# Grouped attention in a new order on all engines of one Trainium2 core

## The chip, the core and the metric

One NeuronCore of one Trainium2 chip runs the whole program. The metric is the device time of one execution in microseconds (us). The core has five engines with a queue each: PE (matrix products and transposes), DVE (vector work), ACT (activations and copies), POOL (vector work and indexed DMAs) and SP (DMA issue). Each takes its own instructions in order; semaphores tie the queues together.

## What is computed

Four layers of attention and feed-forward follow one another over 2048 tokens of width 256. The change touches only the last attention, the grouped one of layer 3 (16 query heads, 4 key and value heads of 64, 77 context tokens). Cut to what matters:

```python
h = _layernorm(x)
Q = rope(h @ Wq)                      # 16 heads of 64
K, V = rope(ctx @ Wk), ctx @ Wv       # 4 heads, each used by 4 query heads
scores = Q @ K.T * 64**-0.5 + rel_pos_bias[:, |i - j|]
x = x + (softmax(scores) @ V).reshape(...) @ Wo
x = x + experts(_layernorm(x))        # 8 experts, one per token, 320 places each
```

## The kernel before, in words

`attn_gqa` holds this attention as one stage. Tokens are cut into 16 tiles of 128 (`NT` is 16, `HALF` is 8). `K` and `V @ Wo` were prepared earlier (`KB`, `VW`), so that a tile needs these links:

- ln: layer norm of a tile, then `lnT`, two transposes on PE, and `lnT_copy` on ACT;
- `queries`: 128x1024 products into two PSUM banks, as two halves of 512 columns;
- `rope` on DVE (three operations from PSUM into `t1`, `t2`), the addition into `qr` on POOL, `q_transpose` (8 transposes on PE), `qT_copy` (two copies on ACT);
- `scores` on PE, `shift` on DVE (adds the bias, takes the maximum of each head, subtracts it), `exps` on ACT, `sums` on DVE (sum of each head and the reciprocal `rden`), the multiplication by `rden` on POOL (`p_ok`);
- `prob_transpose` on PE (ten transposes in three groups of 4, 4 and 2, through the two banks of `ring`), `pT_copy` on ACT, `output` on PE (ten products of `pT` with `VW` into `bank_y`), `residual` on DVE (adds `bank_y` into x, `x_ok`), and `bn_stats` for the next layer norm.

Beside that, DVE adds the results of the previous experts into tiles ahead of their use (`add_experts`), computes variances for groups of four tiles (`variance`, `inverse`; ACT takes the square root in `deviation`), and from tile 8 on prepares the next layer's routing: the normalised tiles `lnk` (`route`), and `first_expert`, `first_slot` and `slots` (`places`). PE has its share of this in `route` (transposes of `lnk`, logits, ranks), and `keep_warm` issues matrix products whose results nobody reads.

Nothing is scheduled by a program: each engine's function `step(t, q)` is an order written out by hand, called for t up to `NT`, in which tiles t-1 to t+7 are worked on at different links. In the step of PE before, these are `scores(t)`, `prob_transpose(t-1)`, `lnT(t+2)`, `output(t-1)`, `q_transpose(t+1)`, `route(t)`, `queries(t+2)`. "Step t" below is the stretch of PE from the first product of `scores(t)` to the first of `scores(t+1)`.

## Time and profile before

| | us |
|---|---|
| median of 3 runs (lowest, highest) | 1019.61 (1019.53, 1022.49) |
| span of the profiled execution | 1018.8 |
| the grouped attention in it | from 573.0 to 806.9 |
| PE busy over the span | 905.3 (89%) |
| DVE busy over the span | 722.6 (71%) |
| ACT busy over the span | 379.2 (37%) |
| POOL busy over the span | 376.2 (37%) |

The span runs from the first to the last instruction of one execution that the profiler recorded. What that same execution took as a whole is not given; the median of the runs lies 0.8 above the span. The lines L... are those of the kernel before. In a timeline, a row gives the start, the length of the group, engine, line, operation, the names written and read, and in brackets for how long the engine had sat idle and what ended it; of a group of several (x8) the ends are modelled, so that distances between starts are the safer reading. The trace counts an f32 product of PE twice (8 products are x16), a transpose once.

### The profile page before, as it was taken

What the parts mean: (1) busy time and instruction counts of PE and PEld (TensorE: products, weight loads), DVE (VectorE), ACT (ScalarE), POOL (GpSimd) and SP (SyncE); (2) the same over time, 40 slices, a digit from 0 to 9 for tenths busy, and PEclk for the clock granted to TensorE, in tenths of its full rate; (3) what the DMA queues carried; (4) which work ended last, traced back from release to release, by engine and by line L of the source; (5) the groups of instructions that cost most, each with busy time, mean ns of one, the idle gap of its engine ahead of it and who ended that gap; (6) DMA issues with size and microseconds to landing.
All of it is one profiled execution on the core that took longest, in us unless ns stands there. A gap on an engine that the chain in (4) does not pass through costs nothing. (4 is left out here: it accounts for less than half of the span.)

```text
span 1018.8 us, 17183 instructions
## 1 busy us (share of the span) xinstructions
PE 905.3 (89%) x5832; PEld 642.5 (63%) x5832; DVE 722.6 (71%) x1632; ACT 379.2 (37%) x862; POOL 376.2 (37%) x279
## 2 busy tenths in 40 slices
PE   2899989999889976868899889999999839999997
PEld 2788743444478864733578467776767517777787
DVE  6799968887699979878377799999989731222221
ACT  3466640000156556844355143434343303122222
POOL 1676404333577623427355223333324410110111
PEclk9999999999999997979999999999999959999999
DMA  7100079999200009002465651111111284624200
GB/s 224 40 1 0 1 223 306 318 324 310 115 1 1 0 2 270 2 27 106 135 197 166 207 173 51 50 50 31 45 50 40 73 313 168 207 89 163 92 12 20
DMA packets 87258, 117.16 MB, mean 115 GB/s; under 512 B 12464, under 2 KB 75949, under 8 KB 86781
## 3 DMA queue, kind: packets, MB, share of 16 engines
q1 hardware_dynamic: 77455, 88.15, 28.5%
q10 hardware_dynamic: 4408, 15.46, 4.3%
q0 software_dynamic: 5328, 12.70, 3.5%
q8 instruction: 38, 0.62, 0.3%
q14 instruction: 29, 0.24, 0.1%
HBM read 68.08 MB, written 50.16 MB: 116 GB/s over the span
## 5 line engine op out<-in xcount | busy, mean ns | idle before, releaser
L1016 PE MATMUL psum<-m_W,lnT 128*128 128x512 f32 x256 | 114.3, 599 | 1.2 <-DVE acc L928 1.2
L410 POOL TENSOR_TENSOR prob<-prob,a_rden 128x1232 f32<-128x1232 f32 x30 | 67.4, 2248 | 59.8 <-DVE a_rden L506 59.8
L1016 PEld LDWEIGHTS psum<-m_W,lnT 128*128 128x128 f32 x256 | 47.3, 190 | 59.5 <-issue 55.9
L2884 ACT ACTIVATE prob<-psum,x_b 128x320 f32<-128x320 f32 x64 | 33.7, 527 | 124.3 <-PE psum L2938 124.3
L2554 PE MATMUL psum<-g_VW,pT 128*128 128x256 f32 (+1 forms) x320 | 72.9, 383 | 1.8 <-ACT pT L2449 1.0
L2938 PE MATMUL psum<-x_xT,x_w 128*128 128x320 f32 x256 | 72.7, 444 | 1.3 <-DVE x_xT L2811 1.3
L1001 POOL TENSOR_TENSOR m_masked<-m_rel,m_mrow 128x1232 f32<-128x1232 f32 x16 | 42.3, 2644 | 82.9 <-DMA masked_bias<-m_masked 62.2
L2744 POOL DMA_INDIRECT out_x<-x_yt,x_X x20 | 19.8, 992 | 140.8 <-DVE x_yt L2825 140.8
L2554 PEld LDWEIGHTS psum<-g_VW,pT 128*128 128x128 f32 (+1 forms) x320 | 59.6, 190 | 12.2 <-issue 4.6
L2938 PEld LDWEIGHTS psum<-x_xT,x_w 128*128 128x128 f32 x256 | 49.6, 195 | 22.9 <-issue 4.4
L2221 POOL TENSOR_TENSOR g_qr<-g_t 128x1024 f32<-128x1024 f32 x15 | 35.4, 2359 | 76.0 <-DVE g_t L2298 76.0
L2228 POOL TENSOR_TENSOR prob<-prob,g_rden 128x1232 f32<-128x1232 f32 x15 | 33.7, 2248 | 73.8 <-DVE g_rden L2334 73.8
L2505 PE MATMUL psum<-g_Wq,lnT 128*128 128x512 f32 x128 | 57.9, 595 | 0.5 <-ACT lnT L2427 0.5
L2951 PE MATMUL psum<-x_w,prob 128*128 128x256 f32 x256 | 56.6, 379 | 0.0
L1389 POOL DMA_INDIRECT routed_results<-pT,m_idx x39 | 38.4, 984 | 39.4 <-DVE pT L1722 21.6
L401 POOL TENSOR_SCALAR ln<-x_tiles,mean,rstd 128x256 f32<-128x256 f32 x32 | 41.5, 1299 | 28.7 <-DVE rstd L433 27.0
L2951 PEld LDWEIGHTS psum<-x_w,prob 128*128 128x128 f32 x256 | 48.1, 190 | 6.1
L472 DVE TENSOR_TENSOR prob<-psum,mx 128x616 f32<-128x616 f32 x64 | 48.2, 795 | 3.0
L466 DVE TENSOR_REDUCE mx<-psum 128x16 f32<-128x1232 f32 x32 | 45.6, 1424 | 4.6 <-PE psum L632 3.6
L931 DVE SCALAR_TENSOR_TENSOR acc<-psum,gates,acc 128x256 f32<-128x256 f32 x96 | 40.4, 477 | 9.7 <-PE psum L1016 9.7
L2822 DVE TENSOR_TENSOR x_yt<-psum,x_b 128x256 f32<-128x256 f32 (+1 forms) x24 | 10.2, 424 | 52.3 <-PE psum L2951 41.3
L110 PE MATMUL psum<-RQ,identb 128*128 128x512 bf16 x135 | 32.5, 396 | 15.7 <-DMA expert_rows<-x_tiles,acc 12.8
(463 smaller groups left out, 2108.1 us busy)
## 6 DMA issues: line engine op xcount, KB each, us to landing
routed_rows<-hole SPq DMA_DIRECT2D x8, 2210.0 KB, 33.9
masked_bias<-m_masked ACTq DMA_DIRECT2D x16, 616.0 KB, 7.4
g_bias<-masked_bias SPq DMA_DIRECT2D x16, 616.0 KB, 3.8
x_w<-in_L_ffn_w SPq DMA_DIRECT2D x16, 512.0 KB, 4.6
x_w<-in_L_ffn_w SPq DMA_DIRECT2D x8, 1024.0 KB, 7.8
m_xb<-routed_rows SPq DMA_DIRECT2D x39, 130.0 KB, 2.2
...
expert_rows<-hole SPq DMA_DIRECT2D x1, 4680.0 KB, 33.5
```

Of the source, the lines that this page charges most:

```text
L401: nc.gpsimd.tensor_scalar(c.ln[b][:, :], xt(c, i), mean_of(c, i), rstd_of(c, i), ALU.subtract, ALU.mult).then_inc(ln_ok, 1)
L410: nc.gpsimd.tensor_tensor(heads(c.prob[b]), heads(c.prob[b]), rden[b][:, :].unsqueeze(2).to_broadcast([P, H, SK]), ALU.mult).then_inc(norm ...
L466: nv.reduce_max(c.mx[:, :].rearrange("p (r h) -> p r h", r=GROUPS), sview.rearrange("p r (h k) -> p r h k", k=SK), AX).then_inc(mx_ok, 1)
L472: nv.tensor_tensor(c.prob[b].rearrange("p (r h k) -> p r h k", r=GROUPS, k=SK)[:, r], sview[:, r].rearrange("p r (h k) -> p r h k", k=SK), ...
L931: ins = nv.scalar_tensor_tensor(out=c.acc[o][:, :], in0=src, scalar=gate, in1=c.acc[o][:, :], op0=ALU.mult, op1=ALU.add)
L1001: nc.gpsimd.tensor_tensor(masked[i % 2][:, :, :], rel[i // 2 % 2][:, :, :], mrow[:, i % 2, :].unsqueeze(1).to_broadcast([P, HB, SK]), ALU. ...
L1016: last = nt.matmul(c.ps[p][:, :], c.lnT[b][:, k * P:(k + 1) * P], W[:, k, p * 512:(p + 1) * 512], start=(k == 0), stop=(k == KC - 1))
L1389: ng.indirect_dma_start(out=c.yd2, out_offset=bass.IndirectOffsetOnAxis(ap=idx[:, b % RING:b % RING + 1], axis=0), in_=yb[:, b % YR, :], i ...
L2505: last = nt.matmul(c.ps[3 + u][:, :], c.lnT[b][:, k * P:(k + 1) * P], Wq[:, k, u * 512:(u + 1) * 512], start=(k == 0), stop=(k == KC - 1))
L2554: last = nt.matmul(bank_y[:, 0:D], c.pT[b][0:w, j * P:(j + 1) * P], VW[0:w, i // HALF, j, :], start=(j == 0), stop=(j == NB - 1))
L2938: last = nt.matmul(c.ps[2 + m % 4][:, 0:CAP], w1[b][:, k, m * P:(m + 1) * P], xT[b][:, k, :], start=(k == 0), stop=(k == KC - 1))
L2951: last = nt.matmul(c.ps[6 + ch % 2][:, 0:D], hT[b][:, m, r * P:(r + 1) * P], w2[b][:, m, :], start=(m == 0), stop=(m == MH - 1))
```

## The change

Everything lies in `attn_gqa`. The work per tile stays the same but for three pieces: the layer norm of a tile moves from DVE to ACT (with `shifts`, minus mean times rstd, computed per group on DVE); of the 16 heads, the first 8 (`FUSED`) are no longer shifted by DVE but by ACT's exponential itself, one head at a time, which also gives their sums; and the orders of all engines are written anew. The deepest links start a step earlier (`queries(t+2)` is followed by `rope(t+2)` in the same step, layer norm and `lnT` are those of t+3), and `residual` runs a step later (`finished(t-2)`).

```diff
@@ DVE: step @@
+        def finished(i):
+
+            residual(i, i % 2)
+            dve.wait_ge(s["x_ok"], i + 1)
+            nv.tensor_copy(c.gap[:, i % 2:i % 2 + 1], c.ones[:, 0:1])
+            stats = nv.bn_stats(bst_of(c, i), xt(c, tile(i)))
+            if i + 2 in (HALF + 1, HALF + 5):
+                chain(stats)
+                variance(group_of((i + 2 - HALF) // 4)[1], s["r_ve_ok"])
+
         def step(t, q):
             b = q % 2
-            if inside(t + 1):
-                rope(t + 1, 1 - b)
+            if inside(t + 3) and t % 4 == 1:
+                inverse(GROUP_OF[t + 3])
+            if inside(t - 2):
+                finished(t - 2)
             if inside(t):
                 shift(t, q)
-            if inside(t + 7):
+            if inside(t + 2):
+                rope(t + 2, b)
+            if t >= -1 and inside(t + 7):
                 add_experts(range(4, 7) if t < 0 else (t + 7,))
             route(t)
             if inside(t):
                 sums(t, b)
-            if inside(t - 1):
-                residual(t - 1, 1 - b)
-                dve.wait_ge(s["x_ok"], t)
-            if inside(t + 3):
-                if t % 4 == 1:
-                    inverse(GROUP_OF[t + 3])
-                layer_norm(t + 3, 1 - b)
-            if inside(t - 1):
-                nv.tensor_copy(c.gap[:, b:b + 1], c.ones[:, 0:1])
-                stats = nv.bn_stats(bst_of(c, t - 1), xt(c, tile(t - 1)))
-                if t in (HALF, HALF + 4):
-                    chain(stats)
+            if t == NT:
+                finished(t - 1)
             if t % 4 == 0 and inside(t + 7):
                 variance(slice(*TILE_GROUPS[GROUP_OF[t + 7]]), s["ve_ok"])
-            if t in (HALF, HALF + 4):
-                variance(group_of((t - HALF) // 4)[1], s["r_ve_ok"])
             places(t)
-        for t in range(-1, NT + 1):
+        for t in range(-2, NT + 1):
             step(t, t % 4)
 
@@ ACT: exponentials @@
+        def exps(t, b, first, last):
+            rest = c.prob[b][:, FUSED * SK:HB * SK]
+            act.wait_ge(s["links"], 2 * t + 1)
+            for h in range(first, last):
+                p = c.prob[b][:, h * SK:(h + 1) * SK]
+                ins = na.activation(p, p, ACT.Exp, bias=c.mx[:, h:h + 1], accum_out=c.den[:, h:h + 1])
+                if h == FUSED - 1:
+                    ins.then_inc(s["fused_ok"], 1)
+                if h == OPENING - 1:
+                    act.wait_ge(s["shifted"], t + 1)
+                    na.activation(rest, rest, ACT.Exp).then_inc(s["exp_ok"], 1)
@@ ACT: step @@
-                deviation(GROUP_OF[t + 7])
-            if t in (HALF, HALF + 4):
+            if inside(t + 3):
+                layer_norm(t + 3, 1 - b)
+            if t in (HALF + 1, HALF + 5):
                 u = (t - HALF) // 4
                 _, ones8, _ = group_of(u)
                 act.wait_ge(s["r_ve_ok"], u + 1)
                 na.activation(c.std[:, ones8], c.ve[:, ones8], ACT.Sqrt).then_inc(s["r_std_ok"], 1)
                 na.activation(spare[:, :], c.ones[:, 0:1], ACT.Exp)
-        step(-2, 2)
+            if inside(t + 1):
+                qT_copy(t + 1, 1 - b)
+            if inside(t - 1):
+                pT_copy(t - 1, 1 - b, 0)
+            if inside(t):
+                exps(t, b, 0, OPENING)
+            if inside(t - 1):
+                pT_copy(t - 1, 1 - b, 1)
+            if inside(t):
+                exps(t, b, OPENING, FUSED)
+            if inside(t - 1):
+                pT_copy(t - 1, 1 - b, 2)
+            route(t)
+            if inside(t + 3):
+                lnT_copy(t + 3, 1 - b)
+            if t % 4 == 0 and inside(t + 7):
+                deviation(GROUP_OF[t + 7])
+        deviation(0)
+        step(-3, 1)
         deviation(1)
@@ PE: step @@
                 pe.wait_ge(s["s_used"], NT)
                 pe_ranks(c, r, 1, c.ps[0]).then_inc(s["r_pre_ps"], 1)
+            early = t == 0
+            if inside(t + 1) and not early:
+                q_transpose(t + 1, 1 - b)
+            if inside(t + 2):
+                queries(t + 2, b, 0)
+            if t == NT:
+                keep_warm(c, c.ps[3], 2)
             if inside(t - 1):
                 if t - 1 in (0, HALF):
                     pe.wait_ge(vw_in[t // HALF], 16 * 2)
-                if t == NT:
-                    keep_warm(c, c.ps[3], 2)
-                prob_transpose(t - 1, 1 - b)
+                prob_transpose(t - 1, 1 - b, 0)
+            if inside(t + 2):
+                queries(t + 2, b, 1)
+            if inside(t + 1) and early:
+                q_transpose(t + 1, 1 - b)
+            if inside(t - 1):
+                prob_transpose(t - 1, 1 - b, 1)
             if t == HALF + 7:
                 pe.wait_ge(s["r_lgT_ok"], 2)
                 pe_logits_back(c, r, 1, c.ps[4]).then_inc(s["r_back_ps"], 1)
-            if inside(t + 2):
-                lnT(t + 2, b)
             if inside(t - 1):
-                output(t - 1, 1 - b)
-            if inside(t + 1):
-                q_transpose(t + 1, 1 - b)
+                output(t - 1, 1 - b, 0)
+                prob_transpose(t - 1, 1 - b, 2)
             route(t)
-            if inside(t + 2):
-                queries(t + 2, b)
+            if inside(t - 1):
+                output(t - 1, 1 - b, 1)
+            if inside(t + 3):
+                lnT(t + 3, 1 - b)
+            if inside(t - 1):
+                output(t - 1, 1 - b, 2)
             back(t)
             if t == NT - 2:
                 keep_warm(c, c.ps[0], 10)
```

Further hunks: POOL adds `qr` for tile t+2 instead of t+1, and DVE does so itself for tiles 0 and 1 instead of tile 0 alone; the last shift and sum cover heads 8 to 15 only; and `output(t-1, u)` waits for the copy of its own part u of `pT`, where before all ten products waited for the last copy. `output(i, 0)` waits, as before, for `x_ok` of the tile before it.

How the orders move is shown at three places. PE, a regular step before (`g_KB` is `scores`, `prob` is `prob_transpose`, `ln` is `lnT`, `g_VW` is `output`, `g_qr` is `q_transpose`, `g_Wq` is `queries`), up to the next step's first row:

```order
-L2527 MATMUL psum<-g_KB,g_qT 128x154 x8
-L2544 MATMUL psum<-ident,prob 128x128 x9
-L2544 MATMUL psum<-ident,prob 80x128
-L2497 MATMUL psum<-ident,ln 128x128 x2
-L2554 MATMUL psum<-g_VW,pT 128x256 x10
-L2518 MATMUL psum<-ident,g_qr 128x128 x8
-L2505 MATMUL psum<-g_Wq,lnT 128x512 x4
-L2527 MATMUL psum<-g_KB,g_qT 128x154 x8
```

and the same in the change, where the transposes of `prob`, the halves of the queries and the parts of the output alternate:

```order
+L2548 MATMUL psum<-g_KB,g_qT 128x154 x8
+L2539 MATMUL psum<-ident,g_qr 128x128 x8
+L2525 MATMUL psum<-g_Wq,lnT 128x512 x2
+L2564 MATMUL psum<-ident,prob 128x128 x4
+L2525 MATMUL psum<-g_Wq,lnT 128x512 x2
+L2564 MATMUL psum<-ident,prob 128x128 x4
+L2574 MATMUL psum<-g_VW,pT 128x256 x4
+L2564 MATMUL psum<-ident,prob 128x128
+L2564 MATMUL psum<-ident,prob 80x128
+L2574 MATMUL psum<-g_VW,pT 128x256 x4
+L2517 MATMUL psum<-ident,ln 128x128 x2
+L2574 MATMUL psum<-g_VW,pT 128x256 x2
+L2548 MATMUL psum<-g_KB,g_qT 128x154 x8
```

The transposes of `qr` moved from behind `output` to right behind `scores`; ten products on `g_VW` in one piece became 4, 4 and 2 with other work between them.

DVE in the change, the end of a step whose number is a multiple of four and the start of the next (`den` is `sums`, `bst` to `var_eps` is `variance`, `g_shifts` ends `inverse`, the last row begins `shift`):

```order
+L2331 TENSOR_REDUCE den<-prob 128x8
+L2333 RECIPROCAL g_rden<-den 128x16
+L2261 TENSOR_TENSOR mean<-bst 128x4
+L2262 TENSOR_TENSOR var_eps<-bst 128x4
+L2263 TENSOR_TENSOR rstd<-bst 128x4
+L2264 TENSOR_SCALAR mean<-mean 128x4
+L2265 SCALAR_TENSOR_TENSOR var_eps<-var_eps 128x4
+L2267 SCALAR_TENSOR_TENSOR var_eps<-rstd,var_eps 128x4
+L2269 TENSOR_SCALAR var_eps<-var_eps 128x4
+L2275 RECIPROCAL rstd<-std 128x4
+L2276 SCALAR_TENSOR_TENSOR g_shifts<-mean,rstd 128x4
+L2314 TENSOR_TENSOR prob<-psum,g_bias 128x924
```

Before, `residual`, the reciprocal of the earlier group and the layer norm on `ln` stood between `g_rden` and `variance`; now `variance` follows at once, and `inverse` stands ahead of the next `shift` instead of at that step's end.

DVE in the change, the end of the stage (`prob<-prob,g_rden` scales the last tile, `L1157` to `L1187` are `first_slot` and `slots`, the rows on `psum` that write `x_tiles` are `residual`):

```order
+L2337 TENSOR_TENSOR prob<-prob,g_rden 128x616 x2
 L1157 COPY acc<-acc 128x8 x2
 L1158 TENSOR_SCALAR acc<-first 128x4
@@ -1115,9 +1102,12 @@
 L1186 TENSOR_TENSOR acc<-acc 128x4
 L1187 TENSOR_TENSOR acc<-acc 128x4
-L2326 TENSOR_TENSOR x_tiles<-x_tiles,psum 128x256
-L2401 COPY gap<-ones 128x1
-L2402 BN_STATS bst<-x_tiles 128x6
+L2325 TENSOR_TENSOR x_tiles<-x_tiles,psum 128x256
+L2384 COPY gap<-ones 128x1
+L2385 BN_STATS bst<-x_tiles 128x6
+L2325 TENSOR_TENSOR x_tiles<-x_tiles,psum 128x256
```

The residual of tile 14, which stood ahead of `L1157`, now stands behind `L1187`, next to that of tile 15.

## Rows read from the trace of the kernel before

**Rows 1.** Windows of stage: length, busy time by engine, clock, DMA share, GB/s.

```profile
613.65:706.03 92.38, 88.80 (x450) 66.73 (x448) 90.20 (x126) 33.51 (x60) 33.81 (x15) 1.00 0.15 49
706.03:789.31 83.28, 78.86 (x429) 59.94 (x428) 74.69 (x140) 33.18 (x68) 28.66 (x14) 1.00 0.13 42
789.31:806.90 17.59, 16.56 (x94) 12.72 (x93) 14.53 (x45) 4.96 (x12) 7.58 (x6) 1.00 0.13 46
```

**Rows 2.** Timeline, PE, tile 4's step: start, duration, idle before it.

```profile
640.00 2.26 PE L2527 MATMUL psum<-g_KB,g_qT 128*128 128x154 f32 x16
642.10 1.04 PE L2544 MATMUL psum<-ident,prob 128*128 128x128 f32 x8
...
643.45 0.44 PE L2544 MATMUL psum<-ident,prob 128*128 128x128 f32 x2 [0.31 <-ACT pT L2446]
...
644.50 4.56 PE L2554 MATMUL psum<-g_VW,pT 128*128 128x256 f32 x20
...
648.90 1.04 PE L2518 MATMUL psum<-ident,g_qr 128*128 128x128 f32 x8
...
649.77 3.60 PE L2505 MATMUL psum<-g_Wq,lnT 128*128 128x512 f32 x8
...
653.21 2.26 PE L2527 MATMUL psum<-g_KB,g_qT 128*128 128x154 f32 x16
```

**Rows 3.** Timeline, the other engines in the same step.

```profile
640.96 1.20 DVE L2296 TENSOR_TENSOR g_t<-psum,g_cos 128x1024 f32<-128x1024 f32 x1
...
643.28 1.11 DVE L2314 TENSOR_TENSOR prob<-psum,g_bias 128x924 f32<-128x924 f32 x1
...
643.44 2.37 POOL L2221 TENSOR_TENSOR g_qr<-g_t 128x1024 f32<-128x1024 f32 x1 [2.94 <-DVE g_t L2298]
...
646.28 1.44 DVE L2321 TENSOR_TENSOR prob<-prob,mx 128x1232 f32<-128x1232 f32 x1
647.63 0.48 DVE L2247 SCALAR_TENSOR_TENSOR x_tiles<-lnk,g_gate,x_tiles 128x256 f32<-128x256 f32 x1
...
649.13 1.44 DVE L2333 TENSOR_REDUCE den<-prob 128x16 f32<-128x1232 f32 x1
649.60 1.08 ACT L2433 ACTIVATE g_qT<-psum 128x512 f32<-128x512 f32 x2 [0.62 <-PE psum L2518]
...
650.60 0.25 DVE L2334 RECIPROCAL g_rden<-den 128x16 f32<-128x16 f32 x1
...
650.93 2.25 POOL L2228 TENSOR_TENSOR prob<-prob,g_rden 128x1232 f32<-128x1232 f32 x1 [5.13 <-DVE g_rden L2334]
```

**Rows 4.** Timeline, ACT, an exponential that also sums, earlier stage.

```profile
406.58 0.42 ACT L1773 ACTIVATE prob<-psum,b_nb,b_rstdA 128x77 f32<-128x77 f32 x1 [0.56 <-DVE b_nb L1480]
...
406.99 0.41 ACT L1773 ACTIVATE prob<-psum,b_nb,b_rstdA 128x77 f32<-128x77 f32 x1
```

**Rows 5.** Groups by line and form: a normalising ACTIVATE, a table load.

```profile
L1749 ACT ACTIVATE pT<-lnk,i_rnd,i_linv 128x256 f32<-128x256 f32 x16 | 8.6, 594 | 5.5 <-DVE i_linv L1423 5.5
...
L2439 ACT ACT_TABLE_LOAD x3 | 3.8, 1283 | 0.1
```

**Rows 6.** Lines L936 and L2279: duration ns min/median/max, first and last start.

```profile
L936 DVE TENSOR_TENSOR x_tiles<-x_tiles,acc x16: 424/726/2850, 156.0 to 269.7; 128x256 f32 x12, 128x256 f32<-128x256 f32 x4
L2279 DVE TENSOR_SCALAR ln<-x_tiles,mean,rstd x16: 320/2158/2166, 575.9 to 758.3; 128x256 f32<-128x256 f32 x16
```

**Rows 7.** Windows: results added for three tiles; the last slot computation.

```profile
585.38:588.99 3.61, 3.48 (x14) 2.08 (x15) 3.54 (x11) 1.09 (x2) 0.00 (x0) 1.00 1.10 350
801.69:805.57 3.88, 3.88 (x19) 3.47 (x20) 3.29 (x20) 0.90 (x3) 0.00 (x0) 1.00 0.00 0
```

**Rows 8.** Timeline, PE, value products of the last tile.

```profile
801.94 4.48 PE L2554 MATMUL psum<-g_VW,pT 128*128 128x256 f32 x20
```

**Rows 9.** Timeline and window, an earlier idle PE and its clock.

```profile
440.97 0.71 PE L1963 MATMUL psum<-ident,prob 128*77 128x128 f32 x2 [3.34 <-ACT prob L1773]
440.00:444.00 4.00, 2.56 (x6) 1.85 (x7) 3.42 (x18) 1.29 (x6) 0.00 (x0) 0.50 0.00 2
```

146 lines of the change are left out of this document (68 added, 78 removed).

## The prediction

> **What bounds the kernel now.** First the windows: in steps 2 to 8, 92.38 us or 13.20 a step, PE is busy for 88.8 and DVE for 90.2 [rows 1]; only PE and DVE can be the bound, and both nearly are. Then PE's timeline in step 4 [rows 2], to see where the step loses time. It starts at 640.00 and 653.21, so it is 13.21 long. Starts that follow each other without a wait give the pace: scores 2.10 (to 642.10), eight transposes 0.87 (648.90 to 649.77, so 0.11 each), output 4.40, queries 3.44 (649.77 to 653.21), and 12 further transposes at 0.11 are 1.31. Sum 12.11; the other 1.10 are waits for ACT's copies, before 643.45 and 644.50. Then the other engines [rows 3]: DVE runs without a gap, rope 2.32, bias and maximum 3.00 (643.28 to 646.28), shift 1.35, one tile of expert results 1.50, sum 1.47. PE is the bound with 1.10 a step to gain; DVE is 0.5 behind it.
>
> What follows counts time from 0 at the first product of `scores(t)`.
>
> **A regular step of the change.** DVE loses the layer norm, 2.16 in most steps [rows 6], and half of shift and sum, about 1.4; 9.3 are left. ACT gains a layer norm (0.59 in a like form) [rows 5] and eight exponentials with sums at 0.41 from start to start [rows 4] for half of the long one, some 3.5 more on an engine that is busy for 33.5 of 92.4 [rows 1]. On PE: `q_transpose` at 2.10, first half of queries at 2.97, transposes of prob at 4.69, second half to 6.84, transposes to 7.28, four products to 9.04, then 9.26, 11.02, 11.24, end at 12.1. ACT: copies of qT from 2.8 (a copy starts 0.7 behind its four transposes) [rows 2, 3], first copy of pT 5.4 to 6.0, two exponentials to 6.8, the other half's exponential to 7.4, second copy from 7.55, six exponentials 8.0 to 10.5, last copy to 10.9, wanted at 11.24. Every PE wait is covered, by 0.3 at the least: 12.11, a gain of 1.10. The loads of the bias on SP wait for the same bias part of `shift` as before and are a step ahead of their use: nothing. The new `shifts` are one small DVE operation per group: nothing where DVE has 2 us to spare.
>
> **The shared access of DVE and POOL.** A DVE operation with two SBUF inputs or the layer norm's tensor_scalar takes its own time alone and POOL's time when POOL is at work: 0.42 against 2.85, and 0.32 against 2.16 [rows 6]. In the step before, POOL's two additions (start 643.44 and 650.93) met DVE's PSUM operations and the layer norm [rows 3]. Now POOL's `qr` addition, 0.1 behind rope's end, meets `add_experts`, and its multiplication by `rden`, 0.33 behind the reciprocal, meets `variance`. I price each meeting at POOL's 2.3 (the distances in rows 3 give 2.36 and 2.25 by the same layer norm's 2.16). The bounds are nothing, if scalar_tensor_tensor doesn't collide, and the full 2.3; I take the full, since the nearest rows, tensor_tensor of x and acc, reach it.
> The Trainium skill ("SBUF — State Buffer", Who interferes with whom) states that a DVE instruction with two SBUF inputs contends with a GpSimd one that reads SBUF, whoever is second waiting for all of the first. By it the sum is the one below; without it 4.5 instead of 16.4. The trace agrees for tensor_tensor; no row has a scalar_tensor_tensor of that kind beside POOL.
>
> In a regular step this pushes the reciprocal to 13.9, `p_ok` to 16.5, or 4.4 of the next step, wanted at 4.69. Still covered; the gain holds in steps 2, 3, 4, 6, 7 and 8.
>
> **Steps after a multiple of four.** In step 4 `variance` waits for POOL (16.5) and ends at 17.4, 5.3 in step 5. ACT stands in `deviation` for it, and `inverse` and the layer norm on ACT now come before `qT_copy`: square root 5.6, inverse 6.0, layer norm 6.6, copy 7.0. PE wants the copy at 4.69: 2.4 lost. A table load of 1.28 [rows 5] and the late shift cost another 1.1 before the last part of output. Step 5 takes 15.6. Steps 2 to 8: six times 12.11 and 15.6 are 88.3 against 92.38: −4.1.
>
> **Start.** Before, step 2 starts at 613.65 [rows 1], and `add_experts` for three tiles runs from 585.38 to 588.99 [rows 7], right behind the addition for tile 0. In the change that addition ends at about the same time, 585.3; PE then needs 0.87 and 3.44 before tile 1's queries are there, at 589.6, and DVE, whose next instruction is rope(1), stands idle until then. Rope 2.3 and its own addition for tile 1 (estimate 1.2, half of POOL's 2.36) end at 593.2, the three tiles' 3.6 at 596.8. Then `shift(0)` with its bias part done at 598.3 and its end at 600.6, rope(2) to 602.9, POOL's addition, behind the scalar_tensor_tensor in flight, to 605.7. PE starts scores(1) at 598.3, has done them by 600.5 and waits 5.2 for that addition, with queries(3) and everything behind in its queue. The scaled prob(0) comes at 610.0; `variance` ends at 610.9, so by the chain above the copy of qT that frees the bank comes at 612.65: a second wait, of 4.3. From there 7.5 of PE work and 1.0 of waits: step 2 starts at 621.2, +7.5.
>
> **Steps 9 to 14**, 83.28 before [rows 1]. Six gains of 1.10, and 0.6 of waits gone that step 9 had: 76.1. Then new waits. Step 9: `inverse` comes at 6.0 as in step 5, and ACT takes the routing's square root before `qT_copy`, behind which all its copies and exponentials stand; `finished(7)` with its variance ends at 7.7, square root, table load and dummy exponential last to 9.4, copy 9.85: 5.2 lost. `lnk` is a tensor_scalar like that of 2.16, meets the `qr` addition and comes at 17.2 to 17.9, while PE, whose `route` now stands ahead of two parts of output, waits from 14.5: 3.1. Step 13 has the same two waits, 1.1 and 2.8 (DVE starts it late, behind `first_expert`), less 0.3. Step 14: `slots` of step 13 meets POOL's multiplication, `shift(14)` starts at 4.9 instead of 2.3, and as the second copy of pT stands behind two exponentials and the half one, PE waits 2.9 and 1.1 there and 0.7 for smaller ones: 4.7. Sum 76.1 + 8.3 + 3.6 + 4.7 = 92.7: +9.4.
>
> **End.** `output(15)` waits for `x_ok` of tile 14. Before, that residual stood ahead of the slot computation and the products began at 801.94 [rows 8]. Now the 3.9 of `first_slot` and `slots` [rows 7] start earlier by the 0.85 of residual and statistics that stood there, end at 804.7, and the residual at 805.2 releases PE: +3.3. With 0.3 for the coupling of copies to exponentials in step 15 the last 17.59 [rows 1] become 21.2: +3.6. The next stage begins behind these residuals and their statistics, so the whole delay is passed on.
>
> **Sum**: 7.5 − 4.1 + 9.4 + 3.6 = +16.4. On the span 1018.8 that gives 1035.2; the median lies 0.8 above the span: 1036.0.
>
> **Rivals.**
> - *The hand-overs are free, 0.14, faster.* Decided at one point: the copy of qT in steps 5, 9 and 13 ready by 4.69, for which `variance` must end 1.75 earlier, at 2.9, so DVE must be ahead of POOL there and at the start. Then 14 steps gain 1.10, less the 3.3 at the end, less a start of 0 to 2: −10 to −12, 1008 to 1010. For it: DVE has 3.4 less to do. Against: rows 6 and the order at the end, which no slack hides.
> - *No collision of scalar_tensor_tensor, 0.20.* Start +2.7, steps 2 to 8 −6.6, step 9 +2.0 instead of +6.6; the lnk and end terms stay: +4.5, 1024; with part of the collisions up to 1028. The 0.08 of it nearest to nothing is no change.
> - *PE's clock falls in the long waits, 0.08, slower still.* An idle of 3.34 stands ahead of 440.97, and the window from 440 has half the clock, 1.2 of 2.4 GHz [rows 9]. Waits of 5.2, 4.3 and 5.2 are longer. If each is followed by 4 us at the half clock that would have been 2 at the full one, +4 to +7: 1040 to 1043.
> The Trainium skill ("TensorE: Matmul & The Clock Gate", Part 1) ties that clock to how busy PE has been; by that rule this rival's 1040 to 1043 is the result, and rows 9 agree.
> - *My walk, 0.58*, 1028 to 1042.
>
> **Numbers.** Predicted 1036. The likeliest case spans 1028 to 1042 and 1024 is the next; from 1020 to 1043, 0.8 and a little more is held, the free hand-overs are left out. Slower 0.58 + 0.08 + 0.12 = 0.78, within 0.3% (3.1 us, about what a measurement tells from no change) 0.08, faster 0.14.
>
> **What would show it.** In the changed profile: regular steps of 12.1 to 12.4 between first products of scores; step 2 starting near 621 behind two PE waits of 4 to 5 us, released by POOL's `qr` and ACT's qT; steps 5 and 9 of 15 and 20, with `variance` operations stretched to 2 us; an idle PE of 3 us in front of the last tile's output, released by DVE. It is wrong if steps 5, 9 and 13 are as short as their neighbours, if regular steps stay at 13, or if the start is not later than 613.65.

## The result and the profile after

The changed kernel takes 1038.01 us (median of 4 runs, 1037.68 to 1041.87), the kernel before 1020.17 in its runs beside it: ratio 1.0175, 95% interval 1.0152 to 1.0198. The forecast was 1036.

The profiled execution has a span of 1035.9, against 1018.8. From the first expert sum of the stage to the barrier behind it 236.3 us have become 254.0, that is +17.7, and the difference of the medians is +17.8. Ahead of the stage this execution happened to be 2.5 longer and behind it 3.1 shorter, in code that is the same.

The stage in four stretches, cut at the first products of scores(0), of step 2, of step 9 and of scores(15), and at the end of the last residual. The windows of the changed kernel; the columns are length, then busy time and count of PE, PE's weight loads, DVE, ACT and POOL, then granted clock, DMA share, GB/s:

```profile
592.26:622.68 30.42, 22.35 (x100) 15.35 (x99) 29.49 (x44) 17.06 (x52) 7.28 (x3) 0.89 0.30 92
622.68:709.49 86.81, 84.91 (x449) 65.91 (x448) 80.13 (x114) 50.24 (x178) 33.39 (x14) 1.00 0.16 52
709.49:804.62 95.13, 81.80 (x427) 61.92 (x426) 70.47 (x146) 48.84 (x168) 31.04 (x17) 0.95 0.12 38
804.62:827.04 22.42, 18.14 (x94) 13.89 (x93) 11.89 (x38) 6.86 (x26) 4.18 (x5) 0.92 0.09 30
```

Steps 2 to 8 took 92.38 and steps 9 to 14 83.28 before [rows 1]; they are 5.6 shorter and 11.9 longer. In the first of them PE is now busy for 98%. The start and the last tile are longer, and the granted clock, which was 1.00 in the stage's steps [rows 1], is below 1.00 in three of the four.

**A regular step.** PE's timeline of step 3, where rows 2 have step 4 of the kernel before:

```profile
634.73 2.26 PE L2548 MATMUL psum<-g_KB,g_qT 128*128 128x154 f32 x16
...
637.70 1.88 PE L2525 MATMUL psum<-g_Wq,lnT 128*128 128x512 f32 x4
639.42 0.60 PE L2564 MATMUL psum<-ident,prob 128*128 128x128 f32 x4
...
642.01 1.89 PE L2574 MATMUL psum<-g_VW,pT 128*128 128x256 f32 x8
...
646.77 0.29 PE L2548 MATMUL psum<-g_KB,g_qT 128*128 128x154 f32 x1
```

None of its rows has a bracket, those left out either: PE waits for nothing, and the step takes 12.04. Steps 2, 3, 4, 6, 7 and 8 are all 12.04 or 12.05. Step 5 is 14.53; there PE waits for ACT's copy of qT:

```profile
661.79 1.88 PE L2525 MATMUL psum<-g_Wq,lnT 128*128 128x512 f32 x4
665.42 0.63 PE L2564 MATMUL psum<-ident,prob 128*128 128x128 f32 x4 [1.75 <-ACT g_qT L2438]
```

From start to start this is 3.63, against 1.72 in step 3: 1.9 are lost here, and 0.6 in the rest of the step.

**The collisions.** DVE's groups; the mean of one instruction in ns stands behind the busy time:

```profile
L2250 DVE SCALAR_TENSOR_TENSOR x_tiles<-lnT_all,g_gate,x_tiles 128x256 f32<-128x256 f32 x16 | 25.1, 1592 | 0.4
L2250 DVE SCALAR_TENSOR_TENSOR x_tiles<-lnk,g_gate,x_tiles 128x256 f32<-128x256 f32 x16 | 7.3, 477 | 4.8 <-DMA lnT_all<-routed_results 4.8
L2264 DVE TENSOR_SCALAR mean<-mean 128x4 f32<-128x4 f32 x4 | 6.6, 1660 | 0.1
```

The two halves of `add_experts` are the same operation on the same size. The first, still ahead of POOL's addition, takes 0.48; the second, beside it, takes 2.45 in 9 of 16 cases. In `variance` a TENSOR_SCALAR of 128x4 takes up to 2.16.

**The start.** PE's and DVE's timelines in step 1:

```profile
601.16 2.33 PE L2548 MATMUL psum<-g_KB,g_qT 128*128 128x154 f32 x16 [0.56 <-DVE prob L2316]
608.30 1.97 PE L2539 MATMUL psum<-ident,g_qr 128*128 128x128 f32 x8 [4.81 <-POOL g_qr L2224]
610.06 3.34 PE L2525 MATMUL psum<-g_Wq,lnT 128*128 128x512 f32 x4
614.83 0.63 PE L2564 MATMUL psum<-ident,prob 128*128 128x128 f32 x4 [1.43 <-ACT g_qT L2438]
...
592.24 1.23 DVE L2295 TENSOR_TENSOR g_t<-psum,g_cos 128x1024 f32<-128x1024 f32 x1 [4.62 <-PE psum L2525]
...
606.08 2.45 DVE L2250 SCALAR_TENSOR_TENSOR x_tiles<-lnT_all,g_gate,x_tiles 128x256 f32<-128x256 f32 x1
...
610.30 2.15 DVE L2264 TENSOR_SCALAR mean<-mean 128x4 f32<-128x4 f32 x1
```

DVE stands idle for 4.62 ahead of rope(1), with the expert sums of three tiles queued behind it. PE waits 4.81 for POOL and then for ACT's copy. The half of the queries between the two waits takes 3.34 where the same products take 1.88 in step 3: the granted clock is 0.51 there, the lower of its two levels (1.2 of 2.4 GHz), and PE was idle for the 4.81 before.

**Step 9.** ACT, then PE:

```profile
714.22 0.20 ACT L2421 ACTIVATE std<-var_eps 128x4 f32<-128x4 f32 x1 [3.72 <-DVE var_eps L2269]
716.77 0.21 ACT L2484 ACTIVATE std<-var_eps 128x8 f32<-128x8 f32 x1 [1.30 <-DVE var_eps L2269]
717.00 1.28 ACT L2485 ACT_TABLE_LOAD   x1
718.40 1.06 ACT L2438 ACTIVATE g_qT<-psum 128x512 f32<-128x512 f32 x2
...
719.13 1.08 PE L2564 MATMUL psum<-ident,prob 128*128 128x128 f32 x4 [4.78 <-ACT g_qT L2438]
720.00 2.98 PE L2525 MATMUL psum<-g_Wq,lnT 128*128 128x512 f32 x4
728.16 0.99 PE L2586 MATMUL psum<-ident,lnk 128*128 128x128 f32 x6 [2.79 <-DVE lnk L2349]
728.99 3.57 PE L2574 MATMUL psum<-g_VW,pT 128*128 128x256 f32 x8
```

Step 9 takes 24.00. Two waits make 7.6 of it, and behind both PE is slow: 2.98 and 3.57 for what took 1.88 and 1.89.

**The end.** DVE, then PE; rows 8 have the same place before:

```profile
819.55 0.16 DVE L1187 TENSOR_TENSOR acc<-acc 128x4 uint32<-128x4 f32 x1
819.63 0.41 DVE L2325 TENSOR_TENSOR x_tiles<-x_tiles,psum 128x256 f32<-128x256 f32 x1
...
820.10 2.74 PE L2574 MATMUL psum<-g_VW,pT 128*128 128x256 f32 x8 [3.23 <-DVE x_tiles L2325]
```

The last of the slots ends at 819.7 (0.16 behind 819.55), the residual of tile 14 comes behind it, and only then PE may write `bank_y` for tile 15.

**The clock.** Windows on PE behind four of these waits; the last columns are the granted clock, DMA share and GB/s:

```profile
606.00:613.00 7.00, 4.70 (x12) 0.51 0.00 0
718.70:722.10 3.40, 2.97 (x7) 0.52 0.56 186
728.90:732.30 3.40, 3.40 (x10) 0.52 0.00 0
821.00:824.50 3.50, 3.50 (x12) 0.53 0.00 0
```

Each goes with an idle of 2.8 to 4.8 us: it begins in that idle or at most 1.1 behind its end. In the regular steps between the clock is 1.00.

The profiled execution of e5_sqrt below was a disturbed one (span 1044.0), so its steps 9 to 14 are read, and its start, end and sum in the table are compared with nothing.

### The profile page after: what moved, and what is told of

Same layout as the page of the kernel before. It is cut to its first block and busy times, and to the rows that moved or that the text cites. A ratio compares the mean times of both kernels' runs of the same rounds, so it can differ in the third digit from the quotient of the medians.

```text
span 1035.9 us, 17456 instructions
## 1 busy us (share of the span) xinstructions
PE 908.6 (88%) x5832; PEld 646.0 (62%) x5832; DVE 702.9 (68%) x1620; ACT 421.5 (41%) x1133; POOL 374.9 (36%) x278
## 5 line engine op out<-in xcount | busy, mean ns | idle before, releaser
L2574 PE MATMUL psum<-g_VW,pT 128*128 128x256 f32 (+1 forms) x320 | 82.8, 402 | 5.9 <-DVE x_tiles L2325 3.2
L2972 PE MATMUL psum<-x_xT,x_w 128*128 128x320 f32 x256 | 70.6, 434 | 1.3 <-DVE x_xT L2845 1.3
L2525 PE MATMUL psum<-g_Wq,lnT 128*128 128x512 f32 x128 | 62.5, 616 | 0.8 <-ACT lnT L2432 0.5
L1389 POOL DMA_INDIRECT routed_results<-pT,m_idx x39 | 38.4, 984 | 39.1 <-issue 20.8
L110 PE MATMUL psum<-RQ,identb 128*128 128x512 bf16 x135 | 32.5, 396 | 15.6 <-DMA expert_rows<-x_tiles,acc 12.8
L660 PE MATMUL psum<-pT,a_VB 128*32 128x128 f32 x1088 | 42.6, 282 | 3.4 <-ACT pT L555 3.4
```

The lines of the kernel that those rows point to most:

```text
L660: last = nt.matmul(bank_o(i)[g * ROWS:(g + 1) * ROWS, m * P:(m + 1) * P], VB[0:rows, b, j, v0:v0 + ROWS], c.pT[b][0:rows, j * P:(j + 1) * ...
L2525: last = nt.matmul(c.ps[3 + u][:, :], c.lnT[b][:, k * P:(k + 1) * P], Wq[:, k, u * 512:(u + 1) * 512], start=(k == 0), stop=(k == KC - 1))
L2574: last = nt.matmul(bank_y[:, 0:D], c.pT[b][0:w, j * P:(j + 1) * P], VW[0:w, i // HALF, j, :], start=(j == 0), stop=(j == NB - 1))
L2972: last = nt.matmul(c.ps[2 + m % 4][:, 0:CAP], w1[b][:, k, m * P:(m + 1) * P], xT[b][:, k, :], start=(k == 0), stop=(k == KC - 1))
```

## The experiments

Each is the changed kernel with the edit that is shown. The kernel before took 1020.2 to 1025.6 as a median beside them, so kernels are compared by their ratio to it. What the stage did is read from each profile, in the four stretches above ("start" from scores(0) to step 2, "end" from scores(15) to the last residual):

| kernel | ratio (95% interval) | start | 2–8 | 9–14 | end | sum |
|---|---|---|---|---|---|---|
| before | 1 | 23.8 | 92.4 | 83.3 | 17.6 | 217.0 |
| changed | 1.0175 (1.0152–1.0198) | 30.4 | 86.8 | 95.1 | 22.4 | 234.8 |
| e1_tail | 1.0145 (1.0103–1.0188) | 30.4 | 86.8 | 93.6 | 17.9 | 228.7 |
| e2_start | 1.0147 (1.0106–1.0187) | 28.0 | 86.8 | 94.1 | 22.4 | 231.4 |
| e3_variance | 1.0122 (1.0084–1.0160) | 29.0 | 85.4 | 94.2 | 22.4 | 231.1 |
| e4_warm | 1.0193 (1.0153–1.0232) | 30.4 | 86.8 | 93.1 | 22.2 | 232.5 |
| e5_sqrt | 1.0098 (1.0068–1.0128) | 31.6 | 86.8 | 92.0 | 23.5 | 234.0 |
| e6_sqrt_route | 1.0139 (1.0102–1.0177) | 30.4 | 86.8 | 91.3 | 20.8 | 229.3 |
| e7_contiguous | 1.0199 (1.0163–1.0235) | 30.8 | 91.4 | 95.2 | 22.2 | 239.6 |
| e8_residual | 1.0170 (1.0111–1.0228) | 30.4 | 87.1 | 95.2 | 17.9 | 230.6 |
| e9_add_first | 1.0184 (1.0134–1.0234) | 30.4 | 85.3 | 93.8 | 22.4 | 232.0 |
| e10_queries_first | 1.0168 (1.0133–1.0203) | 30.4 | 86.8 | 94.1 | 20.7 | 232.1 |
| e11_combined | 0.9995 (0.9969–1.0021) | 27.4 | 84.9 | 85.8 | 17.9 | 215.9 |
| e12_better | 0.9948 (0.9928–0.9968) | 23.8 | 84.9 | 85.8 | 17.9 | 212.4 |

Two things limit what the ratios tell of single edits. The half-clock pieces come and go from one profile to the next: step 9 is 24.00 in the changed kernel and 22.45 in e1_tail, whose edit does not touch it, and the end is 22.4 in one and 20.7 in e10_queries_first. And the code behind the stage, the same in all, took from 206.4 (changed) to 210.2 (e4_warm) in the profiles. So an effect under 2 us is taken from the steps of the trace, where the waits name their releaser; and in step 9 a difference of total length alone says little, since e1_tail, e2_start and e10_queries_first, whose edits leave it alone, have 22.45, 22.96 and 22.97 there, beside the 24.00. The table also leaves out the stretch from the first expert sum to scores(0): it is 16.7 to 16.9 in nine of the profiles and 18.1 to 18.4 in e2_start, e3_variance, e4_warm, e5_sqrt and e12_better. In these five the granted clock falls in it (0.51 from 583.0 to 586.5 in e12_better, 1.00 over the whole stretch in the changed kernel).

**e1_tail**: the residual of tile 14 ahead of the slots.

```diff
-            if inside(t - 2):
+            if inside(t - 2) and t < NT:
                 finished(t - 2)
...
+            if t == NT - 1:
+                finished(t - 1)
             places(t)
```

> Residual, gap copy and bn_stats of tile 14 run on DVE ahead of the slots of the routing instead of behind them. If the output of tile 15 waits only for that residual: it starts near 817.4 instead of 820.1 in the clock of the changed kernel's profile (behind the last tile's value copies), and from the first product of scores(15) to the end of the last residual it is 2.7 to 4.0 us shorter than the changed kernel's 22.4; median 1034 to 1035.5 against the changed kernel's 1038.0. If the slots and the scatters that follow them bound what comes behind, the stage ends earlier and the stage after it waits by as much: 1037.5 to 1038.5.

PE's timeline at the end:

```profile
813.10 1.97 PE L2576 MATMUL psum<-g_VW,pT 128*128 128x256 f32 x8 [0.40 <-ACT pT L2459]
```

The wait of 3.23 for DVE is gone, one of 0.40 for ACT is left, and the stretch is 17.9, near the 17.6 before the change. The edit gives back 4.5: 2.8 of wait, and 1.7 because the products behind the idle no longer run at half the clock. That split is seen in e10_queries_first, where the wait is 3.22 but the clock did not fall (the first four products take 1.99, where the changed kernel has 2.74), and the end takes 20.7. The ratio fell by 0.003, the stage's whole share would be 0.0044; the interval holds both.

**e2_start**: the expert sums of tiles 4 to 6 ahead of rope(1).

```diff
+            if t == -1:
+                add_experts(range(4, 7))
             if inside(t + 2):
                 rope(t + 2, b)
-            if t >= -1 and inside(t + 7):
-                add_experts(range(4, 7) if t < 0 else (t + 7,))
+            if t >= 0 and inside(t + 7):
+                add_experts((t + 7,))
```

> The expert sums of tiles 4 to 6 on DVE ahead of the rotation of tile 1, in the 4.6 us in which DVE waits for that tile's queries. If the start is bound by DVE's queue: the mask addition of tile 0 starts near 596 instead of 599.5 and step 2 starts 3.0 to 3.7 us earlier; median 1034 to 1035. If the expert results land late, or the chain ACT to PE bounds the start, the rotation of tile 1 moves back by as much as was saved: 1037 to 1039.

The mask addition of tile 0 starts 3.6 after the first scores, where it took 7.3, as the first theory says. Of these 3.6 step 2 gets 2.4, less than the 3.0 of its first theory: behind the second wait, which grew from 1.43 to 2.14, half of the queries now takes 2.71 instead of 1.88.

**e3_variance**: the variance ahead of the head sums.

```diff
+            if t % 4 == 0 and inside(t + 7):
+                variance(slice(*TILE_GROUPS[GROUP_OF[t + 7]]), s["ve_ok"])
             route(t)
             if inside(t):
                 sums(t, b)
...
-            if t % 4 == 0 and inside(t + 7):
-                variance(slice(*TILE_GROUPS[GROUP_OF[t + 7]]), s["ve_ok"])
```

> The variance of the next four tiles ahead of the head sums, no longer beside POOL's multiplication by the reciprocals. If the 2.15 us TENSOR_SCALAR in it is a collision with POOL: it falls to 0.15 to 0.2 in all three places, and the start, step 5 (14.5) and step 9 (24.0) get about 2 us shorter each; 4 to 6.5 in all, median 1031.5 to 1034. If the price is the wait of the small operations themselves, or the variance now meets POOL's addition, nothing is gained: 1037 to 1039.

DVE's group of that line in e3_variance:

```profile
L2264 DVE TENSOR_SCALAR mean<-mean 128x4 f32<-128x4 f32 x4 | 0.7, 171 | 0.1
```

From 1660 ns to 171: the operation itself is short, POOL's multiplication was the price. The start gets 1.4 shorter, step 5 goes from 14.53 to 13.13, step 9 from 24.00 to 23.06: less than the 2 of each that its first theory had.

**e4_warm**: products into free banks fill PE's waits.

```diff
+            if t == 1:
+                keep_warm(c, bank_y, 18)
...
+                if t == HALF + 1:
+                    pe.wait_ge(s["x_ok"], HALF)
+                    keep_warm(c, bank_y, 18)
                 prob_transpose(t - 1, 1 - b, 0)
...
+            if t in (HALF + 1, HALF + 5):
+                keep_warm(c, c.ps[0], 10)
```

> Products whose result nobody reads fill PE's long waits: 18 of 512 columns ahead of the transposes of tile 2's queries in step 1, 18 ahead of the first probability transposes in step 9, 10 ahead of the routing's transposes in steps 9 and 13. No wait is taken away. If the clock of 0.50 behind the waits costs time on the path: the queries' half behind the first wait of step 9 takes 1.9 instead of 2.98, the output behind the second 1.9 instead of 3.57, step 9 is 2 to 3 us shorter and the start 1 to 2; median 1033 to 1036. If the steps are bound by DVE and ACT and PE only fills in: within 1 us of 1038.

PE's timeline in step 1 of e4_warm:

```profile
602.27 3.83 PE L110 MATMUL psum<-RQ,identb 128*128 128x512 bf16 x17
607.02 1.09 PE L2539 MATMUL psum<-ident,g_qr 128*128 128x128 f32 x8 [0.92 <-POOL g_qr L2224]
607.95 1.88 PE L2525 MATMUL psum<-g_Wq,lnT 128*128 128x512 f32 x4
613.55 0.63 PE L2564 MATMUL psum<-ident,prob 128*128 128x128 f32 x4 [3.72 <-ACT g_qT L2438]
```

The clock stays at 1.00 (the queries take 1.88), and the start is 30.42 as without the edit: the second wait grew from 1.43 to 3.72. There the half clock cost nothing, it ran inside a wait for DVE and ACT. In step 9 it did cost: 20.85 instead of 24.00. Step 13 became 16.68 instead of 18.37, but step 14 16.41 instead of 13.63. In step 14 and at the end, which have no fillers, the clock fell in this profile too (0.50 from 795.9 to 799.3 and from 816.4 to 819.8). Over the stage the profile has 2.2 us less (234.8 to 232.5); the time does not show them (ratio 1.0193, and the part behind the stage took 3.8 more in this profile). So the clock is worth at least 2 us in the trace, and whether any of it shows in the time stays open.

**e5_sqrt**: ACT's square root for the routing behind two copies.

```diff
+            if inside(t + 1):
+                qT_copy(t + 1, 1 - b)
+            if inside(t - 1):
+                pT_copy(t - 1, 1 - b, 0)
             if t in (HALF + 1, HALF + 5):
                 u = (t - HALF) // 4
...
                 na.activation(spare[:, :], c.ones[:, 0:1], ACT.Exp)
-            if inside(t + 1):
-                qT_copy(t + 1, 1 - b)
-            if inside(t - 1):
-                pT_copy(t - 1, 1 - b, 0)
```

> In steps 9 and 13 ACT's square root for the routing, with its table loads, stands behind the copies of the transposed queries and of the first probability transposes instead of ahead of them. If ACT's place in the order is what holds PE in step 9: PE's wait of 4.8 us ahead of the first probability transposes falls under 1 us, the clock stays at 1.00 behind it, and the chain moves to the reciprocal behind the square root: step 9 falls from 24.0 (22.5 in e1_tail's profile) to 19 to 21, step 13 (18.4) by 0 to 1; median 1033 to 1036. If the second wait, for the routing's layer norm, grows by what the first one loses: 1037 to 1039.

**e6_sqrt_route**: the same, and PE's `route(t)` moved from between `output(.., 0)` and `output(.., 1)` to behind `output(.., 2)`.

> e5_sqrt, and PE's transposes for the routing (and its logits and ranks) stand at the end of the step, behind the output's products, instead of between their first and second part. If the 2.8 us waits for the layer norm on DVE are a matter of place on PE: they are covered by 3 us of products, and steps 9 and 13 are each 2 to 2.8 us shorter than in e5_sqrt; median 1028 to 1032. If ACT's copies of these transposes, which the next step's scores wait for, end last then: the wait stands ahead of the scores, and the time is within 1 us of e5_sqrt.

PE's timeline of step 9, first of e5_sqrt:

```profile
723.13 0.63 PE L2564 MATMUL psum<-ident,prob 128*128 128x128 f32 x4 [1.75 <-ACT g_qT L2438]
732.57 1.51 PE L2586 MATMUL psum<-ident,lnk 128*128 128x128 f32 x6 [4.71 <-DVE lnk L2349]
```

and of e6_sqrt_route:

```profile
713.01 0.63 PE L2564 MATMUL psum<-ident,prob 128*128 128x128 f32 x4 [1.75 <-ACT g_qT L2438]
...
722.47 0.99 PE L2586 MATMUL psum<-ident,lnk 128*128 128x128 f32 x6 [0.27 <-DVE lnk L2349]
723.93 1.32 PE L2548 MATMUL psum<-g_KB,g_qT 128*128 128x154 f32 x8 [0.47 <-ACT lnT_all L2467]
```

In e5_sqrt the first wait fell from 4.78 to 1.75 and the second grew from 2.79 to 4.71: 1.9 of the 3.0 gained at one was lost at the other. PE is done with the work ahead of the second wait 4.5 earlier in the step, but DVE's layer norm `lnk`, which stands behind the rotation, begins only 2.6 earlier (13.5 instead of 16.1 behind the first product). Only with the transposes at the end too does step 9 fall, to 17.52. But in steps 10, 11 and 12 the late routing stands in front of the next scores (13.56, 13.28 and 14.58, where the changed kernel has 12.71, 12.48 and 13.94), and step 14 grows from 13.63 to 16.95: in all 3.8 less than the changed kernel over steps 9 to 14. The median of e5_sqrt, 1033.3, is in its first theory's range, but step 9 is 21.98 and not 19 to 21; and its ratio is lower than the changed kernel's by 0.0077, or 7.9 us, of which steps 9 to 14 account for 3.1. What the other 4.8 are is not shown, so the steps are relied on and not this ratio. The median of e6_sqrt_route, 1035.6, is not in 1028 to 1032 and, with intervals that overlap, not told from e5_sqrt's: its rival, the wait ahead of the scores, holds for steps 10 to 12.

**e7_contiguous**: the halves and parts of PE's order put together again.

```diff
             if inside(t + 2):
                 queries(t + 2, b, 0)
+                queries(t + 2, b, 1)
...
                 prob_transpose(t - 1, 1 - b, 0)
-            if inside(t + 2):
-                queries(t + 2, b, 1)
...
             if inside(t - 1):
-                output(t - 1, 1 - b, 0)
                 prob_transpose(t - 1, 1 - b, 2)
             route(t)
             if inside(t - 1):
+                output(t - 1, 1 - b, 0)
                 output(t - 1, 1 - b, 1)
```

> PE's halves and parts put together again: both halves of the queries ahead of the probability transposes, the three transposes in a row, then the three parts of the output. All else is the changed kernel's, the fused exponentials and the layer norm on ACT too. If the interleaving is what lets PE run without a wait in a regular step: waits for ACT's copies of 0.5 to 2 us come back and a regular step is 12.6 to 14 instead of 12.05; median 1044 to 1060. If it was the work taken from DVE (the former bound) that made the step shorter: a regular step stays under 12.3, median 1037 to 1041.

PE's timeline in a regular step of e7_contiguous:

```profile
646.58 0.44 PE L2564 MATMUL psum<-ident,prob 128*128 128x128 f32 x2 [0.31 <-ACT pT L2457]
646.86 3.62 PE L2574 MATMUL psum<-g_VW,pT 128*128 128x256 f32 x16
```

A regular step is 12.86, inside the first theory's 12.6 to 14 (the median, 1043.5, lies just under its 1044). Of the 1.15 by which the change shortened it (13.20 to 12.05) the interleaving gives 0.81, all else 0.34. The wait for ACT's copy between the transposes is back. What the interleaving gives without the work taken from DVE was not tried; with DVE only 0.5 a step behind PE before the change, it is likely less.

**e8_residual**: `finished` back to the end of its old step.

```diff
-            if inside(t - 2):
-                finished(t - 2)
...
-            if t == NT:
+            if inside(t - 1):
                 finished(t - 1)
```

> The residual of tile t-1 with its bn_stats (and the routing's variance) again at the end of step t, behind the head sums and ahead of the variances and of the routing's places, instead of at the start of step t+1. In a regular step DVE's order is the same by it, so steps 2, 3, 4, 6, 7 and 8 stay at 12.05 by every theory. If the later place costs where other work of DVE stands between (the end; the routing's variance of step 9 and 13): the end is 2.7 to 4 us shorter and steps 9 and 13 0.5 to 2 us each; median 1031 to 1035. If what stands between is needed first anyway (slots for the scatters, variance for ACT): what one gains the other loses, 1037 to 1039.

PE's row where step 13 begins in e8_residual:

```profile
769.71 2.36 PE L2546 MATMUL psum<-g_KB,g_qT 128*128 128x154 f32 x16 [1.95 <-DVE lg L1137]
```

"A residual a step later" moves nothing in a regular step (12.04 and 12.05): it comes behind the head sums of the same tile either way. The end is 17.9 again. What that gains in the stage is partly paid in step 12, 15.58 instead of 13.94: there the read of the routing's logits, for which the next scores wait, now stands behind a residual that waits for the step's last product. The 0.5 to 2 us expected in steps 9 and 13 did not come (22.35 and 18.38), and the time (1.0170) does not tell the kernel from the changed one.

**e9_add_first**: from step 1 on the expert sums ahead of rope.

```diff
+            if t > 0 and inside(t + 7):
+                add_experts((t + 7,))
             if inside(t + 2):
                 rope(t + 2, b)
-            if t >= -1 and inside(t + 7):
+            if t in (-1, 0):
                 add_experts(range(4, 7) if t < 0 else (t + 7,))
```

> From step 1 on the expert sums of tile t+7 stand on DVE ahead of the rotation of tile t+2 instead of behind it, where POOL's addition of that rotation runs beside them. By the collision theory the second SCALAR_TENSOR_TENSOR falls from 2.45 to 0.48 us in these steps. If PE is the bound of a regular step (12.04 us busy in 12.05), 2 us less on DVE change nothing in steps 2, 3, 4, 6, 7 and 8, and only the places where DVE is waited for gain: steps 5 and 9 by 1 to 2 us each; median 1034 to 1036.5. If DVE still bounds the step together with PE, a regular step falls under 11.9. If the collision only moves to other work of DVE, the time stays within 1 us of 1038.

DVE's group in e9_add_first:

```profile
L2250 DVE SCALAR_TENSOR_TENSOR x_tiles<-lnT_all,g_gate,x_tiles 128x256 f32<-128x256 f32 x16 | 9.4, 606 | 0.4
```

From 1592 ns to 606 (one case still collides, that of step 0), 15.7 us of DVE's time gone, and a regular step stays at 12.05. Only step 5 (14.53 to 13.06) and step 9 (to 22.7, which lies between the 22.45 and 24.00 of kernels with that step unedited) are shorter. The time doesn't tell it from the changed kernel; the stretches have 1.5 less in steps 2 to 8.

**e10_queries_first**: in step 1 both halves of queries(3) ahead of the transposes of tile 2.

```diff
+            if t == 1:
+                queries(t + 2, b, 0)
+                queries(t + 2, b, 1)
             if inside(t + 1) and not early:
                 q_transpose(t + 1, 1 - b)
-            if inside(t + 2):
+            if inside(t + 2) and t != 1:
                 queries(t + 2, b, 0)
...
-            if inside(t + 2):
+            if inside(t + 2) and t != 1:
                 queries(t + 2, b, 1)
```

> In step 1 alone PE computes both halves of the queries of tile 3 ahead of the transposes of tile 2's rotated queries, for which it waits 4.8 us there. If the start is PE's order (queries that could run in the wait stand behind it): the wait falls to 1 us or less and step 2 starts 2.5 to 4 us earlier after the first product of scores(1) (21.5 now); median 1034 to 1036. If the chain POOL's addition, transposes, ACT's copies, probability transposes sets the start: 0 to 1 us.

PE's timeline in step 1 of e10_queries_first, then ACT's, and PE's at the end of the stage:

```profile
607.46 6.72 PE L2525 MATMUL psum<-g_Wq,lnT 128*128 128x512 f32 x8 [2.94 <-ACT lnT L2432]
...
615.85 1.06 PE L2564 MATMUL psum<-ident,prob 128*128 128x128 f32 x8 [0.80 <-ACT g_qT L2438]
...
607.05 0.36 ACT L2432 ACTIVATE lnT<-psum 128x256 f32<-128x256 f32 x1
...
820.09 1.99 PE L2574 MATMUL psum<-g_VW,pT 128*128 128x256 f32 x8 [3.22 <-DVE x_tiles L2325]
```

Not a tenth is gained (21.52 again), as the second theory has it, but its chain is right only at its end. The queries now wait 2.94 for ACT's copy of the transposed layer norm, which stands behind the exponentials of tile 0, and run at half the clock; POOL's addition is done at 609.3, long before the transposes begin at 614.0. Yet the first probability transposes start 13.67 behind the first product of scores(1) here, in the changed kernel and in e4_warm alike, each time released by ACT's copy of qT. That copy stands behind DVE's `variance`, ACT's square root, DVE's `inverse` and ACT's layer norm: this chain sets step 1 here, and what PE does ahead of it does not count.

**e11_combined**: e1_tail, e2_start, e3_variance, e5_sqrt, e9_add_first and e10_queries_first in one, and `route(t)` at the end of PE's step for t = 9 alone.

> All that the runs so far speak for: e1_tail, e2_start, e3_variance, e5_sqrt, e9_add_first and e10_queries_first together, and the routing's transposes at the end of step 9 alone. If the losses are independent, the sum of what they gave: the start 6 us shorter than the changed kernel's 47.1, step 5 by 1.4 to 2.4, steps 9 to 14 by 8 to 10 of 95.1, the end by 4.5 of 22.4: 20 to 23 us less than the changed kernel, median 1014 to 1018, ratio to the kernel before 0.994 to 0.998. If the gains overlap (one wait behind another), 1019 to 1025 and no better than the kernel before.

Steps 9 to 14 are 9.3 shorter than the changed kernel's (step 9 15.67), the end 4.5, steps 2 to 8 2.0, but the start, at 27.4, only 3.0. PE's and ACT's timelines in step 1 of e11_combined:

```profile
609.86 5.40 PE L2529 MATMUL psum<-g_Wq,lnT 128*128 128x512 f32 x8 [2.43 <-ACT lnT L2436]
...
615.79 1.09 ACT L2442 ACTIVATE g_qT<-psum 128x512 f32<-128x512 f32 x2 [2.80 <-PE psum L2543]
```

With the variance out of the way ACT is early, and now the copy of qT waits 2.80 for PE, whose transposes stand behind queries that came late and ran slow: what cost nothing in e10_queries_first costs here. The stage is 18.9 shorter than the changed kernel's and 1.1 shorter than before; the ratio is 0.9995, outside the first theory's range and at the low end of the second's.

**e12_better**: what e10_queries_first showed is mended, on top of e11_combined.

```diff
+            if t >= -1 and t != 0 and inside(t + 7):
+                add_experts(range(4, 8) if t < 0 else (t + 7,))
+            if t in (-1, 4, 8):
+                variance(slice(*TILE_GROUPS[GROUP_OF[max(t, 0) + 7]]), s["ve_ok"])
...
+            if t == 0:
+                lnT_copy(t + 3, 1 - b)
             if inside(t):
                 exps(t, b, 0, OPENING)
...
+            if t in (-1, 4, 8):
+                deviation(GROUP_OF[max(t, 0) + 7])
...
+            if late:
+                route_tiles(t)
```

> e11_combined with three more moves. Tile 7's expert sums, the variance and the standard deviation of tiles 4 to 7 stand a step earlier (step -1), so that two table loads of 1.28 us leave ACT's step 0 and 3.4 us of expert sums and 1 us of variance leave DVE's. ACT copies the transposed layer norm of tile 3 ahead of tile 0's exponentials. In step 13 the routing's transposes go to the end of the step, the ranks stay in the middle. If DVE and ACT set the start, the two steps from the first product of scores(0) to that of scores(2) take 23.5 to 26 us instead of e11's 27.4 (the kernel before: 23.8), and steps 13 and 14 together 29.4 to 30.4 instead of 30.9; in all 2 to 5 us less than e11_combined, whose ratio was 0.9995: ratio 0.995 to 0.998, faster than both kernels. If the longer DVE work of step -1 pushes the rotation of tile 1 by as much as step 0 gains: ratio 0.998 to 1.001.

PE's timeline in step 1 of e12_better:

```profile
608.25 3.60 PE L2529 MATMUL psum<-g_Wq,lnT 128*128 128x512 f32 x8
611.68 1.04 PE L2543 MATMUL psum<-ident,g_qr 128*128 128x128 f32 x8
614.30 1.06 PE L2568 MATMUL psum<-ident,prob 128*128 128x128 f32 x8 [1.58 <-POOL prob L2231]
```

Step 1 takes 14.58 instead of 21.52 (19.21 in e11_combined) and the start is what it was before the change, 23.8; over the whole stage (596.94 to 809.29) the granted clock is 1.00. Steps 13 and 14 together are 30.90 as in e11_combined (30.89), so moving the transposes of step 13 gave nothing. Ratio 0.9948, interval 0.9928 to 0.9968: faster than both kernels.

## Why the prediction was right, step by step

The direction, the sum (+16.4 forecast, +17.7 in the stage) and the places are right. That the time is only 2 us off is in part luck. The slow clock, which the sum did not have, cost 4.9 in this profile (3.2 in step 9, 1.7 at the end). Without it the stage's +17.7 would be +12.8, so that the walk itself is about 3.6 too high: 1.0 at the start, 1.5 in steps 2 to 8, 0.7 in steps 9 to 14, 0.5 at the end.

- **Regular steps.** 12.11 forecast, 12.05 measured, each of PE's waits covered as walked. e7_contiguous shows that, with the lighter load of DVE in place, the interleaved order is the larger part of the gain.
- **The shared access.** Confirmed for scalar_tensor_tensor: 0.48 alone, 2.45 beside POOL, and 0.48 again when moved (e9_add_first). By the Trainium skill ("SBUF — State Buffer", Who interferes with whom) this was expected of two SBUF inputs. The meeting in `variance` cost 2.15 against the priced 2.3, but on a TENSOR_SCALAR of 128x4 and not on the scalar_tensor_tensor behind it. As forecast the collisions cost nothing in a regular step: e9_add_first took 2 us per step off DVE and the step did not move. The rival without this collision is refuted.
- **Steps 2 to 8**, −4.1 forecast, −5.6 measured: step 5 was 14.5 and not 15.6. Both of its terms were over-sized: the wait for the copy of qT cost 1.9 (forecast 2.4), table load and late shift 0.6 (1.1). e3_variance and e9_add_first each take 1.4 to 1.5 out of it, e11_combined, with both, 2.0 (12.57).
- **Start**, +7.5 forecast, +6.5 measured from the first expert sum to step 2 (47.1 against 40.6). The first wait is 4.8 (forecast 5.2), the second 1.4 (4.3), since a half-clock piece of 3.34 filled it; at the full clock it is 3.7 (e4_warm). e2_start and e3_variance show two of its causes, worth 2.4 and 1.4. That the chain through `variance` and ACT's copy of qT sets the second wait is as walked (13.67 in three kernels, e10_queries_first). A third cause was not in the prediction: the copy of tile 3's layer norm stands on ACT behind tile 0's exponentials, and once the variance is out of the way the queries that wait for it hold PE (e11_combined). When that copy and the variance were moved ahead, with the expert sum of tile 7, the start fell by another 3.6 (e12_better against e11_combined; how much each gave is not shown).
- **Steps 9 to 14**, +9.4 forecast, +11.9 measured. Step 9's waits were forecast as 5.2 and 3.1 and are 4.8 and 2.8; step 13's as 1.1 and 2.8 with 0.3 off, and are 1.0 and 2.8. What lies beside them was put at nothing: 3.2 of half clock in step 9, which e4_warm gives back (20.85 there, where the forecast comes to 21.0). In step 13 it is 1.7, but there step 14 is shorter by as much: 18.37 and 13.63, or 16.68 and 15.31 in e10_queries_first, sum 32.0 in both, against 32.4 forecast. In the first the waits of step 14 sum to 1.7 and in the second to 3.4, where the forecast had 4.7: PE's speed only moves the wait from one step to the other. That the two are then bound by DVE's layer norm and slots is argued from the order and was not tried apart.
- **End**, +3.6 forecast, +4.8 measured: the wait is 3.23 (forecast 3.3), the half clock behind it 1.7 more, and nothing where the clock did not fall (20.7 in e6_sqrt_route and e10_queries_first). e1_tail takes 4.5 back.
- **The rival of the falling clock** (0.08) took part, beside the walk and not instead of it: 0.51 to 0.53 behind the waits of 4.81, 4.78, 2.79 and 3.23. Its price of 4 to 7 is borne out by the 4.9 of this profile (in others step 9 is up to 1.6 and the end 1.7 shorter), though only in part where it was looked for: step 9 and the end paid it, while at the start and in step 13 the slow piece lies inside another wait. The time stays under the rival's 1040 because the walk beside it was too high. The Trainium skill's rule ("TensorE: Matmul & The Clock Gate", Part 1), by which the clock hangs on how busy PE was, agrees with e4_warm, where the clock stays at 1.00 in steps 1, 9 and 13, which have fillers, and falls in step 14 and at the end, which have none.
